# Scores of a causal attention on 32-row tiles of the matrix engine: one copy of the keys, row product before column product, value sums and side products at other places of the step

## The reference, cut to what matters

```
y = xn @ W1 + b1
q, k, v = split(y per head, 3)              # (2, 16, 1024, 8)
w = (q @ k^T) / sqrt(8)
w = softmax(w * tril - 1e10 * (1 - tril))   # rows of 1024
out = (w @ v) merged @ W2 + b2
```

## Time and profile before

| | |
|---|---|
| median of 3 runs | 1697.95 us |
| profiled execution | 1706.63 us |
| its span | 1704.9 us (1.7 us less than its time) |
| last attention | about 1354 to 1703 us of the span |
| busy in the whole span | PE 1490.4 us (87%), DVE 1260.4 (74%), ACT 1089.9 (64%), POOL 857.1 (50%) |

### The profile page before, as it was taken

One profiled execution on the slowest core, in us unless ns is written; L12 is line 12 of the kernel. 1 busy time (PEld: TensorE's weight loads), 2 busy tenths in 40 slices (PEclk: granted clock), 3 DMA queues, 4 the chain that ended last, 5 costly groups with the idle time before them and its releaser, 6 DMA issues. The chain is left out here.

```text
span 1704.9 us, 29946 instructions
## 1 busy us (share of the span) xinstructions
PE 1490.4 (87%) x11248; PEld 1197.3 (70%) x11248; DVE 1260.4 (74%) x2770; ACT 1089.9 (64%) x2122; POOL 857.1 (50%) x798
## 2 busy tenths in 40 slices
PE   6999999999999999899848888845999379998997
PEld 4788887888788887687737676834788256666675
DVE  6999999999999999435461677589433887777772
ACT  4888888888888888455445565632444456666665
POOL 4556576667666666720363744624666632233211
PEclk9999999999999999999779999957999699999999
DMA  3656666656666565300044000040465200000000
GB/s 94 124 103 115 106 120 100 120 108 114 115 108 103 99 105 106 87 1 1 18 137 129 26 2 2 2 133 1 112 148 109 64 1 1 2 2 2 2 2 26
DMA packets 334417, 117.09 MB, mean 69 GB/s; under 512 B 281008, under 2 KB 326096, under 8 KB 334144
## 3 DMA queue, kind: packets, MB, share of 16 engines
q1 hardware_dynamic: 323664, 101.54, 29.2%
q0 software_dynamic: 8496, 12.59, 3.4%
q10 hardware_dynamic: 2112, 1.05, 0.2%
HBM read 37.53 MB, written 10.49 MB: 28 GB/s over the span
## 5 line engine op out<-in xcount | busy, mean ns | idle before, releaser
L2135 ACT ACTIVATE ET_a<-PS 128x256 f32<-128x256 f32 (+2 forms) x512 | 220.5, 499 | 114.8 <-PE PS L2028 72.9
L771 POOL TENSOR_TENSOR dl<-XN,dh 128x1024 f16<-128x1024 f32 x86 | 184.9, 2150 | 155.2 <-DVE D L743 79.7
L205 PE MATMUL PS<-xh,yh 128*128 128x512 f32 x512 | 215.5, 421 | 6.6 <-ACT XNT L608 3.8
L206 PE MATMUL PS<-xl,yh 128*128 128x512 f32 x512 | 204.0, 398 | 0.0
L207 PE MATMUL PS<-xh,yl 128*128 128x512 f32 x512 | 202.8, 396 | 0.0
L608 ACT ACTIVATE G<-PS,nm 128x1024 f32<-128x1024 f32 x128 | 143.0, 1117 | 53.4 <-DVE nm L693 37.9
L608 ACT ACTIVATE XNT<-PS,nm 128x1024 f32<-128x1024 f32 x128 | 143.1, 1118 | 52.3 <-DVE nm L693 41.0
L687 DVE TENSOR_REDUCE nm<-PS 128x1 f32<-128x1024 f32 x128 | 156.6, 1223 | 15.7 <-PE PS L207 13.8
L689 DVE TENSOR_REDUCE nm<-PS 128x1 f32<-128x1024 f32 x128 | 156.0, 1219 | 4.7 <-PE PS L207 1.0
L205 PE MATMUL PS<-dth,xnh 128*128 128x256 f16 x512 | 141.0, 275 | 12.0 <-DVE zl L697 12.0
L2323 DVE CUSTOM_DVE_ANT_0 PS<-PS,mk 128x256 f32<-128x256 f32 (+3 forms) x256 | 128.2, 516 | 30.6 <-PE PS L2007 30.2
(11 more groups left out here) (461 smaller groups left out, 4091.1 us busy)
## 6 DMA issues: line engine op xcount, KB each, us to landing
e_wg<-in_WgT SPq DMA_DIRECT2D x16, 256.0 KB
e_wu<-in_WuT SPq DMA_DIRECT2D x16, 256.0 KB
e_wd<-in_WdT SPq DMA_DIRECT2D x16, 256.0 KB
dth<-dh SPq DMA_TRANSPOSE x128, 3.2
dtl<-dl SPq DMA_TRANSPOSE x128, 3.2
m_x_rows<-m_xs SPq DMA_DIRECT2D x1, 1472.0 KB, 4.9
m_xs<-m_x_rows SPq DMA_DIRECT2D x5, 256.0 KB, 4.8
m_y_rows<-m_xs SPq DMA_DIRECT2D x5, 256.0 KB, 2.3
```

What stands on the lines that cost most here:

```text
L205: e.matmul(o, l[0], r[0], start=start, stop=False)
L206: e.matmul(o, l[0], r[1], start=False, stop=False)
L771: e.tensor_tensor(self.dl[:, g % 4, :], self.D[g % 3], self.dh[:, g % 4, :], SUB).then_inc(*self.d_low.up(g))
L2135: e.activation(dst, src, ACT.Exp, scale=self.SC, bias=0.0).then_inc(*self.ex.up(it))
```

## The change

- The keys of a quad stay in one tile `KA`, like the queries; the four spread copies, `spread_odd` and ScalarE's `spread` are gone for this attention. VectorE writes `KA` where it wrote `hm`.
- Row and column products contract the head's 32 partitions alone, with `tile_position=(32 * hh, 0)`. Their sizes in columns are as before.
- In a slot the row product comes before the column product. The column products lag by 70 slots, five whole steps, so that row and column product share slots 0 to 11; the row product is head x's, the column product head x-5's, so the two lie on different row tiles.
- The order of the row parts: the first halves go earlier, so that the second half can take the first one's result as the initial value of its minimum. The joining operation L2328 and its signal are gone.
- Value sums at slots 4 and 10; the first part waits only for the first cut. ScalarE takes the sums out at slot 12 instead of 6.
- Side products: "max" at slots 1 and 5; projections at (hh 1) slots 1 and 8, (hh 2) slot 0, (hh 3) slot 1; "give" at slot 8.

```diff
@@ __init__
-        self.KH = [[sb(f"KH{n}_{i}", [128, 1024], F32R) for i in range(4)] for n in range(3)]
+        if kind == 3:
+            self.KA = sb("KA", [128, 3, 1024], F32R)
+        else:
+            self.KH = [[sb(f"KH{n}_{i}", [128, 1024], F32R) for i in range(4)] for n in range(3)]
...
-                self.rparts += [(i, 0, cut, True)] * (cut > 0) + [(i, cut, w_, False)]
+                if cut == 0:
+                    self.rparts += [(i, 0, w_, False)]
+                else:
+                    firsts.append((i, 0, cut, True))
+                    seconds.append((i, cut, w_, False))
...
+            self.rparts += [firsts[0], firsts[1], seconds[0], firsts[2], seconds[1], firsts[3], seconds[2], seconds[3]]
...
-        self.AV_AT = (0, 4) if kind == 3 else (11, 12)
-        self.lag = 63 if kind == 3 else 70
+        self.AV_AT = (4, 10) if kind == 3 else (11, 12)
+        self.lag = 70
...
-                m += [("max", n - 1, c) for c in range(2)]
-            if n + 1 < self.NQ and hh in (1, 2):
-                m += [("project", n + 1, w_, hh - 1) for w_ in (1, 0)]
+                m += [(1, ("max", n - 1, 0)), (5, ("max", n - 1, 1))]
+            if n + 1 < self.NQ:
+                m += {1: [(1, ("project", n + 1, 1, 0)), (8, ("project", n + 1, 0, 0))], 2: [(0, ("project", n + 1, 1, 1))],
+                      3: [(1, ("project", n + 1, 0, 1))]}.get(hh, [])
             if x - 7 >= 1 and (x - 7) % 2 and x - 7 < NH:
-                m += [("give", x - 7)]
+                m += [(8, ("give", x - 7))]
...
@@ pool
-            for ck in range(2):
-                self.spread_odd(e, q, ("project", 0, 1, ck))
             for x in range(self.NH + 5):
-                n, hh = divmod(x, 4)
-                if hh in (1, 2) and n + 1 < self.NQ:
-                    self.spread_odd(e, q, ("project", n + 1, 1, hh - 1))
...
@@ pe: row
-                t = e.matmul(o[:, 0:wd], qs[:, 128 * i:128 * i + 128], kh[:, c0:c0 + wd], start=True, stop=True)
+                r = slice(32 * hh, 32 * hh + 32)
+                t = e.matmul(o[:, 0:wd], qs[r, 128 * i:128 * i + 128], kh[r, c0:c0 + wd], start=True, stop=True, tile_position=(32 * hh, 0))
@@ pe: col
-                t = e.matmul(o[:, 0:wd], kh[:, 128 * jj:128 * jj + 128], qs[:, q1 - wd:q1], start=True, stop=True)
+                r = slice(32 * hh, 32 * hh + 32)
+                t = e.matmul(o[:, 0:wd], kh[r, 128 * jj:128 * jj + 128], qs[r, q1 - wd:q1], start=True, stop=True, tile_position=(32 * hh, 0))
@@ pe: sums
+            q.wait_ge(self.cut, (x, part if self.kind == 3 else 1))
             if part == 0:
-                q.wait_ge(self.cut, (x, 1))
...
@@ pe: the steps
+            if self.kind == 3 and j in self.at and x < self.NH:
+                row(x, self.at[j])
             if m in self.at and 0 <= y < self.NH:
                 col(y, self.at[m])
-            if j in self.at and x < self.NH:
+            if self.kind == 1 and j in self.at and x < self.NH:
                 row(x, self.at[j])
@@ act
-            if j == (6 if self.kind == 3 else 13) and 0 <= x - 6 < self.NH and x % 2:
+            if j == (12 if self.kind == 3 else 13) and 0 <= x - 6 < self.NH and x % 2:
                 take_out(x - 6)
@@ dve: row
+                    least = 3e38
+                    if c0:
+                        least = self.P2[:, n % 2, i - 4, hh:hh + 1]
+                        q.wait_ge(self.top, ("row", x, self.rparts.index((i, 0, c0, True))))
                     e.tensor_tensor_reduce(out=o[:, 0:c1 - c0], in0=o[:, 0:c1 - c0], in1=w.mk[:, 512 - (c1 - c0):512], scale=-1.0,
-                                           scalar=3e38, op0=ADD, op1=MIN, accum_out=dst).then_inc(*self.top.up(it))
-                if j == self.nr - 1:
-                    m4 = M[:, 4:8, col].rearrange("p i c -> p (i c)")
-                    q.wait_ge(self.top, it)
-                    e.tensor_tensor(m4, m4, self.P2[:, n % 2, :, hh], MIN).then_inc(*self.top.up(("both", x)))
+                                           scalar=least, op0=ADD, op1=MIN, accum_out=dst).then_inc(*self.top.up(it))
```

More of the change, by code:

```diff
@@ L1663, in __init__ @@
             self.rparts, self.cparts = [], []
+            firsts, seconds = [], []
             for i in range(8):
@@ L1702, in __init__ @@
             if hh == 0 and 1 <= n <= self.NQ:
-                m += [("max", n - 1, c) for c in range(2)]
-            if n + 1 < self.NQ and hh in (1, 2):
-                m += [("project", n + 1, w_, hh - 1) for w_ in (1, 0)]
+                m += [(1, ("max", n - 1, 0)), (5, ("max", n - 1, 1))]
+            if n + 1 < self.NQ:
+                m += {1: [(1, ("project", n + 1, 1, 0)), (8, ("project", n + 1, 0, 0))], 2: [(0, ("project", n + 1, 1, 1))],
+                      3: [(1, ("project", n + 1, 0, 1))]}.get(hh, [])
             if x - 7 >= 1 and (x - 7) % 2 and x - 7 < NH:
-                m += [("give", x - 7)]
+                m += [(8, ("give", x - 7))]
             if x in (33, 35):
-                m += [("fin", (x - 33) // 2), ("finp", (x - 33) // 2)]
+                m += [(1, ("fin", (x - 33) // 2)), (4, ("finp", (x - 33) // 2))]
             elif x in (34, 36):
-                m += [("sum", (x - 34) // 2)]
-            for j, what in enumerate(m):
-                self.misc[x, 1 + 3 * j] = what
+                m += [(2, ("sum", (x - 34) // 2))]
+            for j, what in m:
+                self.misc[x, j] = what
         first = [("project", 0, w_, ck) for w_, ck in ((1, 0), (0, 0), (1, 1), (0, 1))]
@@ L1750, in of @@
                 if w_:
-                    k_act.extend([("k", n, ck, 0), ("k", n, ck, 2)] if kind == 1 or n else [])
+                    k_act.extend([("k", n, ck, 0), ("k", n, ck, 2)])
                     k_dve.extend([("k", n, ck, 1), ("k", n, ck, 3)])
@@ L1756, in of @@
                 mi.extend([u + (h,) for h in ("r", 0, 1)])
-        if kind == 3:
-            k_act.extend([("k", 0, ck, hh) for hh in (0, 2) for ck in range(2)])
         for u in use:
@@ L1763, in __init__ @@
         self.mi = k.sig("a_side_done", mi)
-        self.k_act = k.sig("a_k_even", k_act)
-        self.k_dve = k.sig("a_k_odd", k_dve)
+        self.k_act = k.sig("a_k_even", k_act) if kind == 1 else None
+        self.k_dve = k.sig("a_k_odd", k_dve) if kind == 1 else None
         self.zero = k.sig("a_zero", ["scratch"])
@@ L1772, in __init__ @@
         self.row = k.sig("a_row", rows)
-        self.top = k.sig("a_row_max", [y for r in rows for y in ([r] + ([("both", r[1])] if kind == 3 and r[2] == self.nr - 1 else []))])
+        self.top = k.sig("a_row_max", rows)
         self.col = k.sig("a_col", cols)
@@ L1893, in pool @@
                 self.gate.pool_step(e, q, x)
[L1895 to L1903, removed]
     def cut_off(self, e, q, x):
@@ L1941, in maxima @@
             _, n, c = u
-            q.wait_ge(self.top, ("both", 4 * n + 3) if self.kind == 3 else ("row", 4 * n + 3, self.nr - 1))
+            q.wait_ge(self.top, ("row", 4 * n + 3, self.nr - 1))
             o = k.bank(self.side_of[u])
@@ L1992, in row @@
             n, hh, b, qd, h = self.head(x)
-            qs, kh, it = self.QS[n % 3], self.KH[n % 3][hh], ("row", x, j)
+            qs, kh, it = self.QS[n % 3], self.KA[:, n % 3, :] if self.kind == 3 else self.KH[n % 3][hh], ("row", x, j)
             if self.kind == 3:
                 i, c0, c1, first = self.rparts[j]
-                q.wait_ge(self.k_act if hh % 2 == 0 else self.k_dve, ("k", n, (c0 + max(c1 - c0, 256) - 1) // 512, hh))
+                q.wait_ge(self.mi, ("project", n, 1, (c0 + max(c1 - c0, 256) - 1) // 512))
                 q.wait_ge(self.mi, ("project", n, 0, i // 4))
@@ L2017, in col @@
             n, hh, b, qd, h = self.head(x)
-            qs, kh, it = self.QS[n % 3], self.KH[n % 3][hh], ("col", x, j)
+            qs, kh, it = self.QS[n % 3], self.KA[:, n % 3, :] if self.kind == 3 else self.KH[n % 3][hh], ("col", x, j)
             if j == 0:
@@ L2091, in project @@
             high(u, o)
-            spread(u)
+            if self.kind == 1:
+                spread(u)
         def high(u, o):
@@ L2102, in high, with spread @@
             e.activation(hn, o, ACT.Identity, scale=m3[:, w_:w_ + 1], bias=self.bm[:, w_, qd:qd + 1]).then_inc(*self.mi_act.up(u))
-        def spread(u, heads=(0, 2)):
+        def spread(u):
             _, n, w_, ck = u
@@ L2108, in spread @@
                 q.wait_ge(self.mi, u)
-                for hh in heads:
+                for hh in (0, 2):
                     r = slice(32 * hh, 32 * hh + 32)
                     self.k_free(q, n, hh)
[L2112 to L2116, removed]
+                    to = self.KH[n % 3][hh][:, 512 * ck:512 * ck + 512]
+                    e.activation(to[r, :], f(hn[r, :]), ACT.Copy).then_inc(*self.k_act.up(("k", n, ck, hh)))
         def col(x, j):
@@ L2150, in act @@
                 high(self.first[m], k.bank(m))
-            spread(self.first[0], (0,))
             high(self.first[3], k.bank(3))
```

(14 more changed lines are left out.)

## The result

The changed kernel takes 1770.74 us (median of 4 runs, 1761.26 to 1786.83), the one before 1697.53 beside it: ratio 1.0444, 95% interval 1.0366 to 1.0522. It is 73 us slower; 28 us faster was forecast. The profiled execution took 1769.13 us, its span is 1767.4. In the experiments some executions of a kernel show a lower clock and take over 1.5% longer than its fastest; their ratios leave these out.

The account below looks back on a forecast made before the run. VectorE with its waits was taken as the bound. Gains of 11 us (waits), 4 (join), 5 (overlap), 3 (rows alone), 1 (end) and 4 (last quad) made 28 off 1697.95: 1670 us, range 1660 to 1685.

Parts of the forecast that it names:

- the one on the 32-row tiles: Score products on 32-row tiles: time by columns unchanged, some overlap of row and column products; 5 us gained.
- a rival with a chance of 0.08: Clock stays at 1.2 GHz in the stage: 54 us a quad, up to 100 us slower, 1800; chance 0.08.
- the 4 of both ends: Stage's ends: 3 us gained with rows alone, 1 us at the very end from the first value part.
- The overlap: Larger-gain rival: row and column products overlap fully, TensorE always ahead; 26 us more, 1644; chance 0.27.
- A cost for each change of row tile: Rival: each row-tile change in a slot costs TensorE 0.1 us; 28 us slower, less 4, 1722; chance 0.10.
- about 36.5: Forecast us per quad of the changed kernel, of which TensorE needs 33.8; before, a quad took 39.2.
- 3 us at the start: Rows alone at the stage's start: 3 of VectorE's 5.9 idle us go with the copies and joins' waits.
- Nothing is gained in the wait: VectorE's projection waits at the new slots: 4.9 us a quad against 4.8 before.
- 11 us for places: Waits at value sums, projections and row maxima: 1.6 us less a quad, over 6.75 quads 11 us.
- 4 for the join: Joining operation gone from VectorE: 8 us in 32 steps, half given back by initial values from memory.
- 4 for the last quad: Last quad's steps, TensorE-bound at 7.74 us, with the cost of two clock falls in the middle: 4 us gained.
- 1.0 to 1.3 for both: VectorE's waits for ScalarE's part of keys and queries at projections, 1.10 and 1.30 us in the step shown.

## Why the prediction was wrong

**The step that failed** is the one on the 32-row tiles: "a product alone should take its time by columns as before". By columns at a given clock it does: on one row tile 512 columns take 0.42 us at 0.50, where they took 0.23 at the full clock. But the clock is another one. In the term's place, 5 us of gain, stand (1.0444 - 0.9855) x 1698 = 100 us of loss, from the changed kernel with and without tiles. I had this as a rival with a chance of 0.08, arguing from the clock's mean of 0.99 and from one fall behind a pause. Both were rows of full-array work. They showed one fall, behind a pause, and gave no reason why nothing else should lower the clock; for products that use a quarter of the rows the trace had no row, and a chance should have said so.

**The rival's price was right, its sum in part by luck.** At the lower level I had 54 us a quad; the chain shows 53.46. Clock 0.62 means that the stage was at half for (1 - 0.62)/0.5 = 76% of the time, over the quarter from which it had to lose. With its terms, 54 us a quad at half and 36.5 at full, that gives 0.76 x 17.5 x 6.75 = 90 us, less the 28 of gain: 62 us slower. Measured are 73 by the medians, and 62.5 between the two profiled executions. But the parts lie elsewhere, as the first and last starts of row and column products show, before and after:

```profile
L2007 PE MATMUL PS<-KH_a,QS_a x384: 276/388/793, 1354.2 to 1657.0; 128*128 128x512 f32 x96, 128*128 128x384 f32 x64, 128*128 128x256 f32 x32
L2028 PE MATMUL PS<-QS_a,KH_a x384: 274/389/628, 1393.9 to 1689.4; 128*128 128x512 f32 x128, 128*128 128x384 f32 x32, 128*128 128x256 f32 x32
L2001 PE MATMUL PS<-KA_a,QS_a x384: 271/500/792, 1348.1 to 1700.3; 32*128 32x256 f32 x95, 32*128 32x384 f32 x95, 32*128 32x512 f32 x2
L2023 PE MATMUL PS<-QS_a,KA_a x384: 271/517/792, 1387.5 to 1752.2; 32*128 32x512 f32 x128, 32*128 32x384 f32 x32, 32*128 32x256 f32 x32
```

From the first column product to the last row product it is 312.8 us against 263.1, so 50 more, not the 66 that this sum has for the quads (90 less 24, the gain without the 4 of both ends), in part because a share of the time at half is a smaller share of the quads, since a quad is longer there. Behind the last row product it is 67.1 us to the end against 47.9, 19 more, at a clock of 0.64; the rival had no term for that part. (The stage also begins 6 us earlier.)

**The other rivals.** The overlap came (products of one slot start together) and gained nothing here. With 64-row tiles, where the clock mostly holds, a quad takes 36.09 us by the chain, from 1431.00 to 1467.09, against 36.31 on the full array: little, as the forecast had it. It had given VectorE and its waits as the reason. That is argued, not shown: on the full array TensorE is busy 250 of 260 us, and it and VectorE wait for each other. A cost for each change of row tile isn't there; the cost of a change to or from the full array is, at 0.20. So the rule of the Trainium skill (TensorEngine Tiling (Array Packing), Key Properties), a drain where the tiling mode changes and not where the tile does, agrees with the trace: 0.20 us for the one, products starting together or 0.06 us apart for the other.

**The rest of the sum held, its parts did not.** Without the tiles' 5 us the forecast was 23 us of gain; the changed kernel on the full array gains 1707.51 - 1684.03 = 23.5. Its quad takes 36.31 us, where I had about 36.5:

```profile
1477.62 1.01 PE PS L2046 x32
...
1486.00 1.01 PE PS L2046 x32
...
1494.73 1.01 PE PS L2046 x32
...
1503.52 1.01 PE PS L2046 x32
...
1513.93 1.01 PE PS L2046 x32
```

That the total agrees is luck, for its parts were distributed wrongly. The copies, to which I gave 3 us at the start and nothing later (of VectorE's waits at the projections I said "Nothing is gained in the wait"), are 0.88% or 15 us by themselves, more than half of it all. The new places and the join together are 0.44%, 7 us, with copies. I had 11 us for places, 4 for the join, 4 for the last quad. In the kernel before without copies VectorE's waits for the queries' part are 0.8 us at most, for the keys' 1.1; I had taken 1.0 to 1.3 for both.

## What to carry to other kernels

Before small products go to row tiles, look whether TensorE's clock is at its full level now, and price the change at the lower level too: a product that leaves rows unused can cost twice. Try tiles of twice the height too (64 rows kept the clock here), and measure schedule and tiles apart: here the new schedule on the full array, with the copies on GpSimd, was 1.3% faster, and the change with its tiles 4.4% slower. Where a trace has no row of the new kind of work, a rival that rests on it can't be given a small chance.

## What the runs showed of the hardware

- TensorE, busy 259.90 of 260 us, was granted half its clock all that time when score products lay on one 32-row tile (0.50); 0.62 with two tiles side by side, 0.94 with 64-row tiles, 1.00 on the full array, with the same column counts and value sums in between. Rows that only hold zeros do not bring it down (0.99 in the kernel before).
- Value products on 32-column tiles take 0.032 us each at the full clock and 0.058 at the lower one.
- Products on different row tiles start together; two of 256 columns follow each other at 0.06 us. Products on the same row tile come one after the other (0.42 us for 512 columns at half the clock).
- A change between full array and row tile costs 0.20 us at the full clock; a change of the row tile costs nothing that shows.
- An initial value from memory instead of a constant costs VectorE's masked minimum 0.06 us.
